# A graph network on one core: the adjacency build with two chunks of first-layer sums inside it and three places for pairs of fine blocks, where there were four chunks and four places for single blocks

## The reference

```python
N_LAYERS = 4
src, dst = edge_index[0], edge_index[1]
for l in range(N_LAYERS):
    agg = jax.ops.segment_sum(x[src], dst, num_segments=n)
    h = x + agg
    h = jnp.maximum(h @ W1[l] + b1[l], 0.0)
    x = h @ W2[l] + b2[l]
```

## Time and profile before

| | |
|---|---|
| median of three runs | 2471.57 us (2466.25 to 2475.18) |
| the profiled execution's own time | 2474.18 us |
| its span | 2472.4 us |
| TensorE busy | 1455.4 us (59%) |
| VectorE busy | 932.2 us (38%) |
| ScalarE busy | 661.6 us (27%) |
| GpSimd busy | 1390.6 us (56%) |
| first and last step of the build (L998) start at | 74.7 and 353.4 us |
| mean granted TensorE clock over the span | 0.738 of full speed |

### The profile page before, as it was taken

One profiled execution on the slowest core, in us unless ns is written; L12 is line 12 of the kernel. 1 busy time (PEld: TensorE's weight loads), 2 busy tenths in 40 slices (PEclk: granted clock), 3 DMA queues, 4 the chain that ended last, 5 costly groups with the idle time before them and its releaser, 6 DMA issues.

```text
span 2472.4 us, 30875 instructions
## 1 busy us (share of the span) xinstructions
PE 1455.4 (59%) x6416; PEld 929.4 (38%) x6417; DVE 932.2 (38%) x2430; ACT 661.6 (27%) x1868; POOL 1390.6 (56%) x1570
## 2 busy tenths in 40 slices
PE   5578879999987165655656155555544343333334
PEld 3234435445443153443433144334333233333333
DVE  6777763112126833333232443333333222222222
ACT  0466660000013143333333154344443000000000
POOL 1400016420312877777775677777776677777776
PEclk8699989999999576767677576666766565656665
DMA  0000001100035133333233222222222222122221
GB/s 20 27 0 0 0 5 11 9 3 1 8 91 220 39 107 106 106 105 106 88 105 99 69 76 78 68 77 75 78 76 69 59 54 55 53 55 55 54 55 46
DMA packets 120576, 148.93 MB, mean 60 GB/s; under 512 B 74731, under 2 KB 88689, under 8 KB 117314
## 3 DMA queue, kind: packets, MB, share of 16 engines
q0 software_dynamic: 40000, 81.89, 12.7%
q1 hardware_dynamic: 80514, 66.31, 8.3%
HBM read 91.39 MB, written 56.72 MB: 60 GB/s over the span
## 4 chain that ended last, share of the span: by engine, by line
POOL 45%; PE 22%; issue 18%; DVE 7%; ACT 3%; DMA 1%; POOLq 1%; DVEq 1%; ACTq 0%; SPq 0%
POOL adj L834 45%; PE acc L1120 14%; PE acc L998 3%; DVE feat L1677 2%; PE acc L1203 2%; ACT adj L1376 1%; PE acc L1267 1%; PE acc L1052 1%; PE acc L1233 1%; PE acc L982 1%; DMA adj<-table,adj 1%; ACT adj L1457 1%; ACT acc L1380 1%; DVE feat L1673 1%; DVE adj L2026 0%
## 5 line engine op out<-in xcount | busy, mean ns | idle before, releaser
L834 POOL DMA_INDIRECT adj<-table,adj x1248 | 1233.2, 988 | 443.9 <-issue 377.5
L1267 PE MATMUL acc<-adj 128*128 x2640 | 534.9, 379 | 697.6 <-ACT adj L1457 348.5
L1267 PEld LDWEIGHTS acc<-adj 128*128 128x128 f32 x2640 | 482.1, 279 | 778.6 <-issue 778.1
L1663 DVE TENSOR_TENSOR adj<-node_iob,drel 128x384 f32<-128x384 bf16 (+1 forms) x444 | 226.6, 552 | 608.0 <-PE acc L1267 607.7
L1457 ACT ACTIVATE adj<-adj 128x128 f32<-128x128 f32 x832 | 263.1, 389 | 582.8 <-DMA adj<-table,adj 499.0
L1120 PE MATMUL acc<-adj,feat 128*128 (+1 forms) x1800 | 339.8, 350 | 2.2 <-DVE adj L1712 2.2
L784 POOL TENSOR_TENSOR node_rep<-node_rep,compb 128x128 f32<-128x128 f32 x128 | 58.2, 455 | 467.3 <-DMA node_rep<-in_L_gnn_weight_dram 458.6
L1233 PE MATMUL acc<-adj 128*128 128x512 f32 (+2 forms) x400 | 221.6, 714 | 71.2 <-ACT adj L1472 71.2
L1120 PEld LDWEIGHTS acc<-adj,feat 128*128 (+1 forms) x1800 | 156.8, 98 | 178.6 <-issue 7.2
L998 PE MATMUL acc<-feat 128*128 128x400 bf16 x620 | 143.5, 372 | 82.3 <-ACT acc L1380 35.4
L1677 DVE TENSOR_SCALAR feat<-feat,temp 128x400 bf16<-128x400 int16 x620 | 163.8, 331 | 0.0
(11 more groups left out here) (258 smaller groups left out, 1059.4 us busy)
## 6 DMA issues: line engine op xcount, KB each, us to landing
table<-adj SPq DMA_DIRECT2D x50, 512.0 KB, 2.8
table<-adj SPq DMA_DIRECT2D x25, 1024.0 KB, 4.1
adj<-table,adj POOLq DMA_INDIRECT x1250, 2.5
table<-adj SPq DMA_DIRECT2D x25, 64.0 KB, 2.0
adj<-in_x_dram SPq DMA_DIRECT2D x3, 512.0 KB, 6.3
out_dram<-adj SPq DMA_DIRECT2D x24, 64.0 KB, 1.5
wrel<-node_rep SPq DMA_DIRECT2D x16, 64.0 KB, 3.0
adj<-in_L_gnn_W_dram SPq DMA_DIRECT2D x2, 512.0 KB, 5.2
```

The lines of the kernel that those rows point to most:

```text
L834: pool.indirect_dma_start(ring[:, p_, 0:D], None, table, bass.IndirectOffsetOnAxis(ap=gidx[:, p_:p_ + 1], axis=0)).then_inc(msgs_in[u.r][c ...
L1267: last = nc.tensor.matmul(acc[:, bass.ds(blk[s], width)], hot[:, c, j, :], ring_flat[:, bass.ds(place[s], width)], start=False, stop=True, ...
L1663: return nc.vector.tensor_tensor(o, node_iob[:, :].unsqueeze(1).to_broadcast([P, n, P]), drel[:, bass.ds(s, n)].unsqueeze(2).to_broadcast( ...
```

## The change

The program sums chunks 0 and 1 inside the build (`EARLY` is 2), and chunks 2 and 3 directly behind it, ahead of chunks 4 to 6 (150 matmuls, in a loop over the source blocks). PSUM banks 2 to 7 become three places of two banks, and each takes a pair of fine blocks. ScalarE copies and clears a pair with one instruction each. TensorE waits until the pair three numbers back has been cleared. `ends_f` counts the steps of pairs, and the numbers for the places come from a division by three. The identity goes onto blocks 8 to 23 behind the build, where it went onto 16 to 23. The core of the diff:

```diff
-FSLOTS = 4
-TURN = 2 * FSLOTS
+PAIRS = FBLOCKS // 2
+FSLOTS = 3
+TURN = 4 * FSLOTS
-EARLY = 4
+EARLY, FRONT = 2, 4
...
-        fslots = [acc[:, (EARLY + i) * KB:(EARLY + i) * KB + FCOLS] for i in range(FSLOTS)]
+        fslots = [acc[:, (EARLY + i * 2) * KB:(EARLY + i * 2 + 2) * KB].rearrange("p (k c) -> p k c", k=2)[:, :, 0:FCOLS]
+                  for i in range(FSLOTS)]
...
-            for i in range(2):
-                nc.tensor.transpose(acc[0:1, (6 + i) * KB + 384:(6 + i) * KB + 384 + P], ends_f[:, i:i + 1], ident[:, :])
+            nc.tensor.transpose(acc[0:1, 6 * KB + 384:6 * KB + 384 + P], ends_f[:, :], ident[:, :])
...
-                build(IPC - 1, at_, EARLY - 1).then_inc(sum_ready, 1)
+                build(IPC - 1, at_, EARLY - 1)
...
                     if l == 0:
+                        block_sums(0, range(EARLY, FRONT), 0, True)
+                        with pe.Fori(1, BLOCKS - 1) as k:
+                            block_sums(0, range(EARLY, FRONT), k, False)
+                        block_sums(0, range(EARLY, FRONT), BLOCKS - 1, False).then_inc(sum_ready, 1)
                         late(0, 0, 2)
...
             def copy_out(i, r, end):
-                nc.scalar.activation(adj[:, :, bass.ds(i * (TURN * FB) + r * FB, FB)],
-                                     fslots[r % FSLOTS].rearrange("p (h n) -> p h n", n=FB), ACT.Copy).then_inc(flushed, 1)
+                nc.scalar.activation(adj[:, :, bass.ds(i * (TURN * 2 * FB) + r * 2 * FB, 2 * FB)].rearrange("p h (k n) -> p h k n", k=2),
+                                     fslots[r % FSLOTS].rearrange("p k (h n) -> p h k n", n=FB), ACT.Copy).then_inc(flushed, 1)
-                nc.scalar.activation(fslots[r % FSLOTS], zerob[:, 0:FCOLS], ACT.Copy).then_inc(zeroed, 1)
+                nc.scalar.activation(fslots[r % FSLOTS], zerob[:, 0:FCOLS].unsqueeze(1).to_broadcast([P, 2, FCOLS]), ACT.Copy).then_inc(zeroed, 1)
...
-            nc.vector.tensor_copy(block_i[0:1, :], fclamp[0:1, :])
-            for i in range(2):
-                last = nc.vector.tensor_scalar(until[:, i, :], fclamp[:, :], part_io[:, i:i + 1], None, ALU.is_le)
-            link(last)
+            link(nc.vector.tensor_copy(pair_i[:, 0, :], fclamp[:, :]))
+            link(nc.vector.tensor_single_scalar(pair_i[:, 1, :], pair_i[:, 0, :], 1, ALU.arith_shift_right))
+            link(nc.vector.tensor_copy(pair_f[:, :], pair_i[:, 1, :]))
...
-            nc.vector.tensor_reduce(ends_f[:, :], until[:, :, :], AXX, ALU.add)
+            link(nc.vector.tensor_scalar(slot_i[0:1, 0, :], pair_f[0:1, :], 171.0, None, ALU.mult))
+            link(nc.vector.tensor_single_scalar(slot_i[0:1, 1, :], slot_i[0:1, 0, :], 9, ALU.arith_shift_right))
...
+            link(nc.vector.tensor_scalar(fcount[:, :], pair_f[:, :], part_io[:, 0:1], None, ALU.is_le))
+            link(nc.vector.tensor_reduce(ends_f[:, :], fcount[:, :], AXX, ALU.add))
...
-                    dve.wait_ge(flushed, (c + 1) * KB // FB)
+                    dve.wait_ge(flushed, (c + 1) * KB // (2 * FB))
                     add_own(4 * c, 4).then_inc(diag_set, 1)
                     iterations(FIRST_AT + c * IPC, IPC)
```

More of the change, by code:

```diff
@@ L626, in _ @@
             with sp.If(peak_sp > 0):
-                sp.wait_ge(flushed, FBLOCKS)
+                sp.wait_ge(flushed, PAIRS)
                 sp.dma_start(un[:, 0:BLOCKS - 1, :],
@@ L991, in build @@
                     min_val=0, max_val=7 * KB,
-                    skip_runtime_bounds_check_because="a bank of the fine sums times 512; a fine block's number plus 1")
+                    skip_runtime_bounds_check_because="a bank of the fine sums times 512; a pair number plus 1")
                 places, turns_ = vals[0:FPI], vals[FPI:]
@@ L1023, in built @@
             def built():
-                pe.wait_ge(flushed, FBLOCKS)
-                pe.wait_ge(zeroed, FSLOTS + FBLOCKS)
+                pe.wait_ge(flushed, PAIRS)
+                pe.wait_ge(zeroed, FSLOTS + PAIRS)
             def general_sums(z, nodes_first, degrees):
@@ L1105, in general_layers @@
                     pe.sem_inc(sum_ready, 2)
-                    for half in (range(0, EARLY), range(EARLY, CH)):
+                    for half in (range(0, FRONT), range(FRONT, CH)):
                         if l == 0:
@@ L1370, in _ @@
                                      ACT.Copy).then_inc(tiles_set, 1)
-            hold(act, ends_set, 3)
+            hold(act, ends_set, 2)
             def copy_out(i, r, end):
@@ L1385, in load_ends @@
                 return ends
-            with act.Fori(0, FBLOCKS // TURN) as i:
+            with act.Fori(0, PAIRS // TURN) as i:
                 for r, end in enumerate(load_ends(i, TURN)):
                     copy_out(i, r, end)
-            left = FBLOCKS % TURN
-            for r, end in enumerate(load_ends(FBLOCKS // TURN, left - 1) + (FSTEPS,)):
-                copy_out(FBLOCKS // TURN, r, end)
+            left = PAIRS % TURN
+            for r, end in enumerate(load_ends(PAIRS // TURN, left - 1) + (FSTEPS,)):
+                copy_out(PAIRS // TURN, r, end)
             act.wait_ge(bias_in, 32)
             for l in range(LAYERS):
-                for half, chunks in enumerate((range(0, EARLY), range(EARLY, CH))):
+                for half, chunks in enumerate((range(0, FRONT), range(FRONT, CH))):
                     act.wait_ge(sum_ready, l * 2 + (half + 1))
@@ L1708, in build @@
                 dve.wait_ge(fstep_done, FSTEPS + AHEAD)
-                dve.wait_ge(flushed, FBLOCKS)
+                dve.wait_ge(flushed, PAIRS)
                 add_own(4 * EARLY, BLOCKS - 1 - 4 * EARLY)
```

31 lines of the change are left out of this document (14 added, 17 removed).

## The result

The changed kernel takes **2497.64 us** (median of 6 runs, 2495.46 to 2500.21); the kernel before, run beside it, 2470.99 us (6 runs, 2465.27 to 2475.18). The ratio is 1.0112 with a 95% interval of 1.0096 to 1.0128: 26.65 us or 1.1% slower. The forecast was 2498 us.

A forecast was written before the change was run, and what follows sets the result against it. No single engine bounds the build; a TensorE-VectorE loop with 1.9 us idle at iteration starts does. Terms +0.3 - 7.8 + 0 + 0.3 + 1.1 + 32.5 = +26.4 us; median forecast 2498 us, range 2486 to 2516.

The forecast's parts named there:

- The price of the moved sums: Behind the build: 150 matmuls of 512 columns at 0.2166 us each, nothing else running on TensorE, +32.5 us.
- the slow start: Right behind the build: 18 matmuls in 5.60 us, taken to be in both kernels and so given no cost.
- What the build gives back: Iterations 16 to 25 without sums, -6.2 us; the iteration outside a loop moving from 25 to 15, -1.6 us.
- only the tail behind the last group shows: In iterations with sums: 15 sums hide in TensorE's waits for VectorE except the last ones, adding some 0.75 us.
- The pairs: In the build: ScalarE's load falls by a fifth, worth 0 us on the path, bounds -3 and +3.
- The reading of the 1.9 us as TensorE's own: At iteration starts: the idle time is TensorE's branch and loading of 24 registers, not a wait for ScalarE's clear.
- a stop that is always the same: At the starts of iterations 6 and 30: idle 1.89 and 1.94 us, whether the clear ended 0.7 us earlier or not.
- The clock: Rival: iterations 16 to 30, without sums, make the clock fall for good; +46.5 us, 2518 us; chance 0.10.
- The identity and last copy: End of the build: last copy is a pair's, +0.3 us; identity addition 2048 elements wide, +1.1 us.
- The setup: Ahead of the build, on VectorE's chain: operations swapped, 2.4 us gone and 2.8 new, sum +0.3 us, bounds 0 and +1.
- a third of the sums hidden: In the chances: one of two ways to land within 0.3% (7.4 us) of the kernel before; that outcome's chance 0.04.

The follow-up runs named there:

- the spread sums: The kernel before, with six sums behind an iteration's first group and three behind the last (before: three and six): 2734.95 against 2730.58 us, ratio 1.0005.
- The short clear: The kernel before, with ScalarE's clear of each place cut from 400 columns to 16: 2746.83 against 2747.91 us, ratio 0.9998.

## Why the prediction was right

**The price of the moved sums.** Predicted 32.5 us, measured 31.16 (0.21 us each in the kernel without them). It was taken from the next layer's block of the same shape, and TensorE is full there: 37.13 of 37.14 us. The term was 1.3 too high; the prediction held the slow start to be "there in both kernels", but the block of 168 took 36.99 us where 150 x 0.2166 and the old 5.60 make 38.1. What made it shorter is not shown. The Trainium skill ("TensorE: Matmul & The Clock Gate", section "Back-to-back issue gap") gives about 131 ns for a 512-column matmul in a steady stream with its weight load; an estimate from that figure is 20 us for the 150 sums. No run here shows that: all of them show 0.21 to 0.22 us.

**What the build gives back.** Predicted -6.2 and -1.6, measured -5.96 and -1.62. The stretches of the same kernel without sums were the right measure for iterations that would lose theirs. 15 sums of 3.25 us lengthened an iteration by 0.75 only. The prediction's reason, "only the tail behind the last group shows", is wrong in its wording: the spread sums refute it. With sums an iteration is TensorE's own work: steps of 1.04 us for the first group and 0.86 for each of three others, 3.6, 15 sums by 0.217, 3.25, and the stop of 1.9 make the 8.8. Without them TensorE has 5.5 us of it in 7.75 to 8.6, and at least 2.2 us are idle. These the sums filled. This sum is worked out from rows. What supports it: in the earlier trace rows, five iterations with sums leave TensorE 44.40 - 35.72 = 8.7 us idle, 1.7 each, and so nothing beyond the stop; spreading the sums changes nothing; and with four loads an iteration with sums grows to 11.49 us while TensorE's busy time stays near the same (7.34 us against some 7.1). A shorter load in an iteration with sums was not run.

**One rule for three pairs of kernels.** Moving the sums costs what stands behind the build (from the last iteration's start to the first weight product) less what the build's last iteration starts earlier. In the three pairs of traces:

| the kernels | build earlier by | longer behind it by | difference | medians |
|---|---|---|---|---|
| before, after (one load of 24) | 347.26 - 340.99 = 6.3 | 32.6 (31.16 + 1.40) | 26.3 | 26.65 |
| with two loads of 12 | 336.04 - 318.03 = 18.0 | 33.7 (49.27 - 15.54) | 15.7 | 13.9 |
| with four loads of 6 (from the last load) | 406.7 - 380.0 = 26.7 | 34.4 (46.8 - 12.4) | 7.7 | 4.1 |

The price of the sums outside is nearly the same everywhere; the price inside depends on how much of TensorE's time stood idle. What is left between the last two columns, 1.8 and 3.6 us, is within the spread of the runs, which lie up to 17 us apart in one kernel.

**The pairs.** Predicted 0. The sums moved without pairs cost 27.5 us, with them 26.65, and iterations 16 to 25 agree within 0.3 us. The short clear shows the cause: ScalarE has slack. The reading of the 1.9 us as TensorE's own was right; its "branch and the loading of 24 registers" is for 1.617 us the load. Its reason, a stop that is always the same, was partly luck: the two starts that it read had 1.89 and 1.94 us, while the stops run from 0.4 to 1.97 from iteration 2 on. The constant is the 0.34 us from the load's end to the matmul.

**The clock.** Not a rival that came true. In iterations 16 to 25 the mean is 0.83 and their time what was predicted. It does shift small terms: iterations 0 to 5 took 0.84 us longer, with a mean clock of 0.75 in place of 0.84 between 102 and 137 us. Iteration 11, with sums, took 10.38 us (184.30 to 194.68), its first step at the low level; iteration 7 took 10.5 as well, and in the kernel before it was iterations 6 and 7 that took 10.6 and 10.5, so the stretch of 6 to 13 came out the same. The kernels with two loads stand at 0.93 to 1.00. The Trainium skill ("TensorE: Matmul & The Clock Gate", section "A second HAM failure mode: psum-queue depth-cycling") tells of a clock that swings where TensorE idles between groups; the traces agree in that. They do not single out one stop: with sums the clock is 1.00 beside stops of 1.7 us; without sums it is 0.75 to 0.84 with one stop of up to 1.94 us in an iteration, 0.93 to 1.00 with two of some 1.1, and 0.73 again with four of 0.3 to 1.4 (375.37 to 401.86 us above).

**The small terms.** The identity and last copy +1.40, as predicted. The setup +0.45 for 0.3. That the sum came within 0.3 us of the medians' difference is in part luck: the sums' term was 1.3 too high, and iterations 0 to 13 took 0.9 longer, by the clock as far as is seen, which was not in it. One step of the chances was worked out wrongly, though nothing hung on it: a third of the sums hidden, 10.8 us, would have left 15.6 us, more than the 7.4 that a measurement tells from none; it takes 19 of the 32.5 us, more than half.

**What stays open.** Why the stages behind the layers take some 260 to 277 us more on the other chips. They lie in the other three networks: GpSimd's gathers (L834) start at 794.9 us on the first chip and at 797.7 in the kernel with spread sums, and the last starts at 2458.5 and 2715.3, though they are busy 1233 and 1237 us. And the version with two loads was not run on the first chip, though the stretch that it shortens is the same length there.

## What to carry to other kernels

Work that lies inside a loop where its engine waits costs only what it adds to the loop; before moving it out, lay an iteration that has it beside one that has not, and compare that difference with the price of the work alone in a full stretch. An idle time at loop starts whose releaser had ended earlier is the engine's own: look for a register load in its queue, and for a fixed distance from its end to the first matmul, before taking work from the engine that is named. When places are given up for something else, count them again: three pairs were enough here, two pairs cost 40 us.

## What the runs showed of the hardware that was not expected

- Loading registers of TensorE from a tile takes 1.617 us for 24 values, 0.85 for 12, and for 6 either 0.81 or 1.47 (the first and third, and the second and fourth, of four to an iteration; why they differ is not shown). Two loads to an iteration were faster than one here (6.98 us in place of 7.75 to 8.6), four were slower (8.83).
- A load starts without waiting for the matmuls ahead of it to end: where these ran at the low clock, they went on for 0.84 us under it (339.04 to 339.88). The next matmul came 0.34 us behind the load's end.
- The granted clock in iterations without sums was 0.75 to 0.84 with one load of 24, 0.93 to 1.00 with two of 12, and 0.73 with four of 6, though TensorE's matmuls were the same.
- An ACTIVATE of 800 columns takes 0.84 us where two of 400 take 0.97 to 1.02; of 16 columns 0.187.
- The time per sum of 512 columns is 0.21 to 0.22 us in each stretch that TensorE fills.
